# Output projection of the silu experts as three fp16 matmuls, in a pipeline that runs on across images

## What is computed

```python
gates = jnp.einsum('nk,nke->ne', topk_probs, onehot)
h1 = jnp.einsum('nc,ehc->neh', flat, w1)
h3 = jnp.einsum('nc,ehc->neh', flat, w3)
h = jax.nn.silu(h1) * h3
y = jnp.einsum('neh,ech->nec', h, w2)
out = jnp.einsum('ne,nec->nc', gates, y)
```

## Time and profile before

| | us |
|---|---|
| median of 3 runs | 4231.09 (4228.9 to 4235.95) |
| the profiled execution | 4227.69 |
| its span | 4225.8 |
| PE busy | 3397.3 (80%) |
| DVE busy | 2491.0 (59%) |
| ACT busy | 1933.4 (46%) |
| POOL busy | 841.4 (20%) |
| silu activation, x352 | 210.2, 597 ns each |
| product u, x352 | 243.4, 691 ns each |
| gating hg on POOL, x352 | 451.6, 1285 ns each |
| output matmuls, x704 records | 361.5, 597 ns each |

### The profile page before, as it was taken

How to read it: one execution, slowest core, us unless ns; L and a number is a source line. 1 busy time by engine, 2 the same in 40 slices (tenths; PEclk the granted TensorE clock), 3 DMA queues, 4 the chain that set the end, 5 groups by cost and what they waited for, 6 DMA issues and landing times. The chain is left out here.

```text
span 4225.8 us, 66475 instructions
## 1 busy us (share of the span) xinstructions
PE 3397.3 (80%) x24463; PEld 1531.3 (36%) x24463; DVE 2491.0 (59%) x4085; ACT 1933.4 (46%) x2321; POOL 841.4 (20%) x861
## 2 busy tenths in 40 slices
PE   6988777557687777777777777769988649999999
PEld 4655554324211111111111111343476524444444
DVE  3227766365688888888888888334377323333333
ACT  1215666512156666666666666524333223233332
POOL 0001333400000000000000000014400035555555
PEclk9997889778799999999999999869988779999999
DMA  4444544300400000000000000014300022232221
GB/s 138 135 119 94 114 110 109 76 1 23 157 11 15 23 21 15 20 15 25 14 20 14 20 25 5 8 63 150 120 1 0 28 91 80 86 97 83 86 82 47
DMA packets 137544, 247.17 MB, mean 58 GB/s; under 512 B 34808, under 2 KB 47264, under 8 KB 136800
## 3 DMA queue, kind: packets, MB, share of 16 engines
q1 hardware_dynamic: 137312, 243.98, 20.2%
HBM read 171.55 MB, written 56.62 MB: 54 GB/s over the span
## 5 line engine op out<-in xcount | busy, mean ns | idle before, releaser
L1073 DVE TENSOR_REDUCE mxv<-mx_ps 128x1 f32<-128x512 f32 x2048 | 1279.7, 682 | 238.2 <-PE mx_ps L932 238.1
L1048 ACT ACTIVATE PT<-st_ps 128x1024 f32<-128x1024 f32 x1024 | 992.4, 1021 | 447.9 <-PE st_ps L945 442.0
L932 PE MATMUL mx_ps<-KS,QS 24*128 24x512 f16 x2048 | 538.1, 391 | 317.9 <-DVE mxv L1073 300.6
L1916 DVE TENSOR_TENSOR u<-h_ps,s 128x512 f32<-128x512 f32 x352 | 243.4, 691 | 541.5 <-ACT s L1891 495.3
L959 PE MATMUL o_ps<-PT,VA 128*32 128x512 f32 x4096 | 546.4, 605 | 1.1 <-ACT PT L1048 0.9
L1953 POOL TENSOR_TENSOR hg<-u,gb 128x512 f32<-128x512 f32 x352 | 451.6, 1285 | 378.9 <-DVE u L1916 296.6
L1891 ACT ACTIVATE s<-h_ps 128x512 f32<-128x512 f32 x352 | 210.2, 597 | 595.7 <-PE h_ps L1865 595.7
L667 DVE TENSOR_REDUCE mxv<-mx_ps 128x4 f32<-128x512 f32 x512 | 319.8, 683 | 146.4 <-PE mx_ps L542 140.0
L1873 PE MATMUL y_ps<-hg,w 128*128 128x512 f32 x704 | 361.5, 597 | 55.2 <-POOL hg L1953 55.2
L932 PEld LDWEIGHTS mx_ps<-KS,QS 24*128 24x128 f16 x2048 | 137.3, 91 | 568.2 <-DVE mxv L1073 530.8
L945 PE MATMUL st_ps<-QS,KS 26*128 26x512 f16 x2048 | 327.0, 382 | 1.0 <-ACT PT L1048 0.2
(11 more groups left out here) (231 smaller groups left out, 4155.8 us busy)
## 6 DMA issues: line engine op xcount, KB each, us to landing
gb<-g SPq DMA_DIRECT2D x64, 512.0 KB, 3.7
gb<-g SPq DMA_DIRECT2D x16, 2048.0 KB
QK<-qk SPq DMA_DIRECT2D x128, 192.0 KB
qk<-hl SPq DMA_DIRECT2D x80, 256.0 KB, 3.3
RB<-d SPq DMA_DIRECT2D x48, 256.0 KB, 3.5
qk<-hl SPq DMA_DIRECT2D x64, 128.0 KB, 3.3
v<-vs SPq DMA_DIRECT2D x32, 256.0 KB, 3.2
VS<-v SPq DMA_DIRECT2D x32, 256.0 KB, 3.3
```

The source lines that it names most:

```text
L932: nc.tensor.matmul(mx_ps[:, use % 3, :], rows(QS, g // 2, j, STACK)[:, t * C:(t + 1) * C], rows(KS, g // 2, j, STACK)[:, half * HALF:(half ...
L1048: nc.scalar.activation(PT[:, n % 2, 2 * a:2 * a + 2], st_ps[:, a], ACT.Exp, scale=1.0 / SHIFT ** 2).then_inc(st_free[a], 1)
L1073: nc.vector.tensor_reduce(mxv[:, g % 2, j, t, half:half + 1], mx_ps[:, slot], AX.X, ALU.max).then_inc(mx_free, 1)
```

## The change

The fp32 output matmul becomes three fp16 ones. The weights w2, scaled by 256, are split into `w2h` and `w2l` at the stage's start: a scaled copy on ACT and a subtraction on DVE, with w2 passing through the gate buffer, so that SyncE also waits for it before the first gates. The gated values `hg` are split in every step, into `hh`, a cast on ACT two steps later, and `hl`, a subtraction on DVE. `hg` now has two slots, and POOL waits for the subtraction two steps back; `hh` and `hl` have four. PE's output matmuls come four steps after the hidden set (`LAG` = 4). The inner loops have no tail at an image's end any more: what is outstanding of image i - 1 is done in the first steps of image i. So the add of the first half is at n = 27, and that of the second half at n = 5 of the next image. SyncE's loop is the same but for the added wait. The cut diff:

```diff
+W2_UNIT = 2.0 ** 8
-    H_SLOTS, HG_SLOTS, LAG = 2, 4, 2
+    H_SLOTS, P_SLOTS, CAST, LOW, LAG = 2, 4, 2, 2, 4
...
-        w2 = chip.buf(ctx, "w2", [C, CHUNKS, C])
+        w2h, w2l = (chip.buf(ctx, n, [C, CHUNKS, C], F16) for n in ("w2h", "w2l"))
-        hg = chip.buf(ctx, "hg", [C, HG_SLOTS, HALF])
+        hg = chip.buf(ctx, "hg", [C, H_SLOTS, HALF])
+        hh, hl = (chip.buf(ctx, n, [C, P_SLOTS, HALF], F16) for n in ("hh", "hl"))
...
-                sp.dma_start(w2[:].rearrange("p c m -> p (c m)"), dram["m3_w2"]).then_inc(w2_loaded, 16)
+                sp.dma_start(whole(0, 1), dram["m3_w2"]).then_inc(w2_loaded, 16)
                 sp.wait_ge(w_split, 2)
+                sp.wait_ge(w2_split, 1)
...
+                def output(i, n):
+                    s, c = n // CHUNKS, n % CHUNKS
+                    if c == 0:
+                        pe.wait_ge(added, i * 2 + s + 1)
+                    pe.wait_ge(rest, i * PER + n + H_SLOTS + 1)
+                    nc.tensor.matmul(y_ps[:, s], w2h[:, c, :], hh[:, n % P_SLOTS], start=(c == 0), stop=False)
+                    nc.tensor.matmul(y_ps[:, s], w2l[:, c, :], hh[:, n % P_SLOTS], start=False, stop=False)
+                    nc.tensor.matmul(y_ps[:, s], w2h[:, c, :], hl[:, n % P_SLOTS], start=False,
+                                     stop=(c == CHUNKS - 1)).then_inc(y_steps, 1)
+
+                def image(i, first):
+                    for n in range(PER):
+                        hidden_rows(i, n)
                         if n >= LAG:
+                            output(i, n - LAG)
+                        elif not first:
+                            output(i - 1, PER + n - LAG)
...
+                def round_hidden(i, n):
+                    act.wait_ge(gated, i * PER + n + H_SLOTS + 1)
+                    act.wait_ge(y_steps, i * PER + n + 1)
+                    nc.scalar.copy(hh[:, n % P_SLOTS], hg[:, n % H_SLOTS]).then_inc(cast, 1)
...
                         nc.scalar.activation(s1[:, n % H_SLOTS], h_ps[:, n % H_SLOTS, 0], ACT.Silu).then_inc(silu_done, 1)
+                        if n >= CAST:
+                            round_hidden(i, n - CAST)
+                        elif not first:
+                            round_hidden(i - 1, PER + n - CAST)
...
+                act.wait_ge(w2_loaded, 16)
+                nc.scalar.activation(w2h[:].rearrange("p c m -> p (c m)"), whole(0, 1), ACT.Copy, scale=W2_UNIT).then_inc(w2_hi, 1)
...
+                def rest_of_hidden(i, n):
+                    v.wait_ge(cast, i * PER + n + 1)
+                    v.wait_ge(y_steps, i * PER + n + 1)
+                    nc.vector.tensor_tensor(hl[:, n % P_SLOTS], hg[:, n % H_SLOTS], hh[:, n % P_SLOTS],
+                                            ALU.subtract).then_inc(rest, 1)
+
+                def add(i, s):
+                    v.wait_ge(y_steps, i * PER + (s * CHUNKS + CHUNKS + P_SLOTS))
+                    at = X[:, i, s * HALF:(s + 1) * HALF]
+                    nc.vector.scalar_tensor_tensor(at, y_ps[:, s], 1 / W2_UNIT, at, ALU.mult, ALU.add).then_inc(added, 1)
...
                         nc.vector.tensor_tensor(u[:, n % H_SLOTS], h_ps[:, n % H_SLOTS, 1], s1[:, n % H_SLOTS],
                                                 ALU.mult).then_inc(hidden, 1)
+                        if n >= LOW:
+                            rest_of_hidden(i, n - LOW)
+                        elif not first:
+                            rest_of_hidden(i - 1, PER + n - LOW)
...
+                        if n == LAG + 1 and not first:
+                            add(i - 1, 1)
                         if n == CHUNKS + LAG + 1:
-                            v.wait_ge(y_steps, i * PER + (CHUNKS + HG_SLOTS))
-                            at = X[:, i, 0:HALF]
-                            nc.vector.tensor_tensor(at, y_ps[:, 0], at, ALU.add).then_inc(added, 1)
-                    v.wait_ge(y_steps, i * PER + (PER + HG_SLOTS))
-                    at = X[:, i, HALF:N]
-                    nc.vector.tensor_tensor(at, y_ps[:, 1], at, ALU.add).then_inc(added, 1)
+                            add(i, 0)
...
+                v.wait_ge(w2_hi, 1)
+                nc.vector.scalar_tensor_tensor(w2l[:].rearrange("p c m -> p (c m)"), whole(0, 1), W2_UNIT,
+                                               w2h[:].rearrange("p c m -> p (c m)"), ALU.mult, ALU.subtract).then_inc(w2_split, 1)
...
                         pool.wait_ge(hidden, i * PER + n + H_SLOTS + 1)
-                        pool.wait_ge(y_steps, i * PER + n + 1)
-                        nc.gpsimd.tensor_tensor(hg[:, n % HG_SLOTS], u[:, n % H_SLOTS], gb[:, s, tile],
+                        pool.wait_ge(rest, i * PER + n + 1)
+                        nc.gpsimd.tensor_tensor(hg[:, n % H_SLOTS], u[:, n % H_SLOTS], gb[:, s, tile],
```

More of the change, by code:

```diff
@@ L1791, in silu_experts @@
     GB = E + len(MIXED)
-    H_SLOTS, HG_SLOTS, LAG = 2, 4, 2
+    H_SLOTS, P_SLOTS, CAST, LOW, LAG = 2, 4, 2, 2, 4
     PER = 2 * CHUNKS
-    assert PER % HG_SLOTS == 0
+    assert PER % P_SLOTS == 0
     with chip.stage() as ctx:
         wh, wl = (chip.buf(ctx, n, [C, 2, CHUNKS, C], F16) for n in ("wh", "wl"))
-        w2 = chip.buf(ctx, "w2", [C, CHUNKS, C])
+        w2h, w2l = (chip.buf(ctx, n, [C, CHUNKS, C], F16) for n in ("w2h", "w2l"))
         xh, xs, xl = (chip.buf(ctx, n, [C, 2, HALF], F16) for n in ("xh", "xs", "xl"))
@@ L1807, in silu_experts, with whole @@
         w_rest = [chip.sem("w_rest") for _ in range(2)]
-        w2_loaded, h_ready, silu_done, hidden, gated, y_steps, added, stored = (chip.sem(s) for s in (
-            "w2_loaded", "h_ready", "silu_done", "hidden", "gated", "y_steps", "added", "stored"))
+        w2_loaded, w2_hi, w2_split = (chip.sem(s) for s in ("w2_loaded", "w2_hi", "w2_split"))
+        h_ready, silu_done, hidden, gated, cast, rest, y_steps, added, stored = (chip.sem(s) for s in (
+            "h_ready", "silu_done", "hidden", "gated", "cast", "rest", "y_steps", "added", "stored"))
         gb_loaded = [chip.sem("gb_loaded") for _ in range(2)]
-        def whole(n):
-            return gb[:, n].rearrange("p g t -> p (g t)")[:, 0:CHUNKS * C]
+        def whole(n, k=0):
+            return gb[:, n].rearrange("p g t -> p (g t)")[:, k * CHUNKS * C:(k + 1) * CHUNKS * C]
         def flat(part, n):
@@ L1852, in _ @@
             def _(pe):
[L1853 to L1866, removed]
-                        if n >= LAG:
[L1868 to L1874, removed]
@@ L1876, in _, with hidden_rows @@
-                pe.wait_ge(w_split, 2)
-                pe.wait_ge(w2_loaded, 16)
-                with pe.Fori(0, B) as i:
-                    image(i)
+                def hidden_rows(i, n):
+                    s, c = n // CHUNKS, n % CHUNKS
+                    if c == 0:
+                        pe.wait_ge(x_scaled, i * 2 + s + 1)
+                        pe.wait_ge(x_lo, i * 2 + s + 1)
+                    pe.wait_ge(hidden, i * PER + n + 1)
+                    for m in range(2):
+                        out = h_ps[:, n % H_SLOTS, m]
+                        nc.tensor.matmul(out, wh[:, m, c, :], xh[:, s], start=True, stop=False)
+                        nc.tensor.matmul(out, wh[:, m, c, :], xl[:, s], start=False, stop=False)
+                        mm = nc.tensor.matmul(out, wl[:, m, c, :], xs[:, s], start=False, stop=True)
+                    mm.then_inc(h_ready, 1)
@@ new lines, in image @@
+                def image(i, first):
+                    for n in range(PER):
+                        hidden_rows(i, n)
+                        if n >= LAG:
+                            output(i, n - LAG)
+                        elif not first:
+                            output(i - 1, PER + n - LAG)
+                pe.wait_ge(w_split, 2)
+                pe.wait_ge(w2_split, 1)
+                image(0, True)
+                with pe.Fori(1, B) as i:
+                    image(i, False)
@@ L1881, in _ @@
+                for n in range(PER - LAG, PER):
+                    output(B - 1, n)
             @block.scalar
@@ L1886, in high, with image @@
                     nc.scalar.activation(xs[:, s], x, ACT.Copy, scale=1 / LO).then_inc(x_scaled, 1)
-                def image(i, last):
+                def round_hidden(i, n):
+                    act.wait_ge(gated, i * PER + n + H_SLOTS + 1)
+                    act.wait_ge(y_steps, i * PER + n + 1)
+                    nc.scalar.copy(hh[:, n % P_SLOTS], hg[:, n % H_SLOTS]).then_inc(cast, 1)
+                def image(i, first, last):
                     for n in range(PER):
@@ L1899, in _ @@
                     nc.scalar.copy(flat(wh, n), whole(n)).then_inc(w_hi, 1)
+                act.wait_ge(w2_loaded, 16)
+                nc.scalar.activation(w2h[:].rearrange("p c m -> p (c m)"), whole(0, 1), ACT.Copy, scale=W2_UNIT).then_inc(w2_hi, 1)
                 high(0, 0)
-                with act.Fori(0, B - 1) as i:
-                    image(i, False)
-                image(B - 1, True)
```

(30 more changed lines are left out.)

## The result

The changed kernel takes 4303.41 us (median of 4 runs, 4301.27 to 4305.79), the kernel before 4232.1 beside it: a ratio of 1.0173, 95% interval 1.0156 to 1.0189. It is slower, by 71 us. The forecast was 4300, with 4262 to 4322. The profiled execution took 4305.79 with a span of 4303.9; against the span before, 4225.8, that is 78 more.

A forecast was written before the change was run, and what follows sets the result against it. Gate loads and TensorE were candidate bounds; the load recurrence set the pace. First gates at 3444.4, image 1 at 3541.5, 13 halves of 54.5 to 4250.0, end 4297.5: forecast 4300 us, range 4262 to 4322.

The forecast's parts named there:

- The 98.9 us: Image period before the change: 53.9 us of chunks from gates to add, then 45 us of load; said to set the pace.
- The load: Gate load on SyncE's queue, issue to POOL's use: 43.9 us on average; each microsecond of length counts 14 times.
- From the gates to the add: In each half of the changed kernel, the add starts 9.1 us after gates arrive at T.
- The estimate by rows on one engine: Gate load: first DMA engine gets 410 rows plus 64, at 25 GB/s for 2 KB each about 38 us.
- The first gates: Stage start: the subtraction `w2l` delays the first gates by 2.95 us, from 3441.44 to 3444.4.
- Low until T+5: TensorE's clock after its wait of some 10 us: taken as low until 5 us after gates arrive at T.
- The bound for a clock that stays up: At full clock, DVE and POOL excluding each other would set the add at T+8.65; 9 us less in total.
- A new cycle rest, gating, rest costs 1.89 us: DVE and POOL exclude each other each chunk: 0.08 + 1.27 + 0.54 us, just below TensorE's 1.94, so no steady-state cost.
- Rival 1: Faster: gate loads stay hidden and TensorE sets the pace at 1.94 us a chunk; 4133 us, chance 0.05.
- The drain at an image's end: TensorE's drain at each image's end, taken as 3 us beside its 94.7, removed by the change.
- rival 2: A gate load finding its DMA engine empty is much shorter; at 41.2 us the total is 4262 us; chance 0.08.
- Rival 3: Slower still: after each gate arrival DVE and POOL block each other, 33 us more, 4333 us; chance 0.08.

The follow-up runs named there:

- the loads' place in the queue, alone: The changed kernel, with SyncE's reload waiting for POOL's last gating of the half instead of that half's add, the store staying behind the add: 4148.75 us, ratio 0.9804.
- the kernel with the filling: The changed kernel with 38 unused matmuls put in front of hidden sets n = 4 and n = 26 of images 1 to 7: 4298.84 us, ratio 1.0155.
- short loads: The changed kernel, each straddling tile's gate transfer cut into a multiple of 16 rows and a rest: 4120.86 us; again beside the four-slot kernel 4128.76 us.
- four slots: The changed kernel with evenly cut gate loads and `hg` in four slots for two: 4108.97 us, against 4128.76 us with two slots.

## Why the prediction was right

**The mechanism** stands point by point. The recurrence through the gate loads set the pace before, the moved second add made two loads of an image one chain, and each half costs a load and the way from the gates to the add. The part that runs on, alone, gives the full loss; the loads' place in the queue, alone, takes it away; cutting one transfer of fourteen gives back 136 us. That the split is hidden behind the loads is shown by both parts alone. At the restart shown, the chain of waits that the forecast wrote down comes in its order, at most 0.9 us late at each link: set 5 starts 5.9 us after the gates (5.7 taken), `u(5)` 8.7 (7.9), the add 9.9 (9.1).

One reading of the kernel before was off. The 98.9 us closed with the 53.9 us that image 0 takes from its gates to its add. In six of the eight images it is 52.4, as from the 3540.31 of rows 3 to this add:

```profile
3592.76 0.68 DVE L1925 TENSOR_TENSOR X<-y_ps,X 128x512 f32 x1
```

With the 45.4 of the load that recurrence is 97.9 us. It set the pace all the same, since TensorE's 94.7 with the measured drain of 1.9 is 96.6.

**The terms.** The load: 43.9 us taken, 43.5 measured. From the gates to the add: 9.1 taken, 9.9 at the arrival shown and 9.6 on average (54.5 less 43.5 and 1.47). Half an image: 54.5 and 54.5, so these two misses cancel, which is luck. The estimate by rows on one engine, "about 38 us" (38.8 by its own numbers), falls 5 us short of the load measured, and no run shows where those go. The first gates: 3444.4 taken, 3447.8 measured. Of that, the wait for `w2l` was right (3.08 us for 2.95):

```profile
L1978 DVE SCALAR_TENSOR_TENSOR w2l<-gb,w2h 128x2816 f16<-128x2816 f32 x1 | 3.1, 3083 | 0.0
```

The other 3.4 are the stage's start, later by 2.6 in this execution, which the change does not touch, and a first load of 45.6 us instead of 44.8. Image 1 begins 98.5 us after the first gates, not 97.1, and the end comes 48.7 after the last gates, not 47.5. The four add up: 3.4 + 1.5 + 0.3 (the thirteen halves) + 1.2 = 6.4 us between 4297.5 and 4303.9. The median is nearer to its forecast than the span is, 3.4 us, partly by luck: the profiled execution lies 2.4 above the median here and lay 3.4 below it before, and the sum as written gives 4302.8 for the median, which was said as 4300.

**What was mis-sized.** "Low until T+5" for the clock: it was low until T+5 to T+8, at the arrival shown until T+7.2. The bound for a clock that stays up, an add at T+8.65, came out at 8.8 in the kernel with the filling. "A new cycle rest, gating, rest costs 1.89 us ... no cost in steady state": POOL's release takes 0.14 us and not 0.08, and the cycle 1.96, above TensorE's 1.94. Behind the loads that cost nothing. With short loads it was the bound, and together with the operations that DVE has besides it cost 12 us in the stage (700.3 and 688.4). Rival 1's time of 4133 thus had two errors: its halves are 43.4 us, not 42.6, and short loads also shorten the first one, by 27 us. The drain at an image's end was worth 1.9 us rather than 3.

**The rivals.** A load on an empty engine was no shorter (43.5 at fourteen such loads), so rival 2 fell. Rival 3 was there only in part: the rest took 1.06, 1.43 and 0.83 us in the first three steps after the gates, yet the add came less than one microsecond late.

## What to carry to other kernels

Before taking work off an engine, find every recurrence that lies within a few per cent of the present pace, buffer reloads among them: here a chain of 98 us through a load stood beside TensorE's 96.6 us, and little taken from TensorE could show. When a pipeline is made to run on, look at what each moved completion releases. Let a buffer's reload wait for its last reader, not for a later step that happens to imply it. And where the tail of a load shows one DMA engine at work, cut odd row counts into a multiple of 16 and a rest. An effect that is read at one arrival should be read at all of them before it is believed.

## What the runs showed that was not expected

One cut in one of 14 transfers, from 127 rows to 112 and 15, takes 8.7 us off a load of 43.5. With all of them cut, 26 transfers for 14, the first load takes 18.7 us for 45.6.

TensorE's clock did not follow the length of the standing alone. In the kernel with the filling it fell after a standing of 2.2 us at one restart and stayed at 1.00 through 2.8 us at another. In the kernel with one transfer cut it fell at three restarts after 2.2 to 2.5 us and stayed up through 2.3 at another. In the changed kernel it was still at 1.00 in the fourth microsecond of standing at the arrival shown (3594.3 to 3598), and at 0.50 at every restart after 7.5 us or more.

Which of the two excluding engines paid went by who issued first. With two slots DVE's subtraction took 1393 ns and POOL's gating 1284, with four slots 729 and 1656, and the stage was 12 us shorter.
